# A four-layer graph network on one core: batches between layers 0 and 1, segment maxima inside layer 3's first pass, reciprocals inside its second, and one column for ScalarE

## The chip, the cores and the metric

One NeuronCore of one Trainium2 chip. TensorE (PE in the profile), VectorE (DVE), ScalarE (ACT), GpSimd (POOL) and the queues of SyncE (SP) run side by side and wait for each other by semaphores. A name with a q behind it in the profile (DVEq) is that engine's sequencer: the small steps with which it works out an address in a loop or the value of a wait. The metric is the device time of one execution in microseconds (us).

## The reference: what is computed

```python
h = relu(layernorm(x)); x = x + L0(h)     # weighted sums over neighbours, weights from cosines
h = relu(layernorm(x)); x = x + L1(h)     # 8 relations, softmax over each node's edges per relation
h = relu(layernorm(x)); x = x + L2(h)     # gated messages, their sum and maximum, an MLP
h = relu(layernorm(x)); x = x + L3(h)     # 4 heads:

e = leaky_relu(xl[src] + xr[dst], 0.2)                    # xl, xr: (nodes, 4, 64)
score = einsum('ehc,hc->eh', e, att)                      # (100000 edges, 4)
m = segment_max(score, dst)
ex = exp(score - m[dst])
denom = segment_sum(ex, dst)
alpha = ex / maximum(denom[dst], 1e-16)
out = segment_sum(alpha[:, :, None] * xl[src], dst).mean(axis=1) + bias_gat
# then batch norm, an MLP of 256, batch norm
```

There are 3,125 nodes with 64 values and 100,000 edges sorted by destination. All is float32.

## The kernel before

Node i lies on partition i // 25, so that 25 tiles (NT) hold all nodes; they are worked on in five batches (NBATCH) of five tiles (NB). Edge e lies on partition e // 784 (T = 784 columns), and a loop over edges goes over 98 groups (NG) of 8 columns (K). `quads` unrolls six groups, and then a loop has four groups in its body. Nearly all large tiles are parts of one SBUF tensor, `arena`. `Beats` counts the finished instructions of one kind; its `wait` makes the engine wait for the last of them, its `done` is an instruction and that wait, and `step` is the same with one semaphore for all.

**From layer 0 to layer 1.** VectorE copies the neighbour sums out of PSUM (L1857). TensorE turns them, 25 products for each half of the partitions (L1282), into PSUM banks 0 to 3; VectorE waits for both halves, joins all 25 tiles in two instructions (L1862, L1863), normalises all 25 tiles (`norm_relu`, L1660 to L1668, with a square root on ScalarE, L882), and stages the first batch (L1689). Then for each batch TensorE turns it (L1163), ScalarE lifts it to SBUF (L896), TensorE multiplies it (L1177, five products into bank 5 and then five of 512 columns over banks 0 to 4), and VectorE takes the results (`nodes1`, L1877 to L1882) into one tile, tb1. SyncE writes tb1 to HBM (L587), and `nodes1` of the next batch waits for that.

**Layer 3, first pass.** For each group GpSimd issues eight indirect gathers (L714), and for group g it waits for the `relu3` of group g - 4; SyncE loads another tile (L629), ScalarE writes the gathered rows out again (L1089). In `edges3` VectorE fills eight columns (L1775, an instruction with 260 values a column), and between these, two groups behind, multiplies what TensorE added up (`relu3`, L2251, which waits for TensorE; L1347 and L1348) and reduces it (L2258); three groups behind it writes the scores (`score3`, L2266). A line L110 is the value of a `Beats` wait.

**Between the passes** VectorE works alone. `segment_totals` makes running maxima over the 784 columns of each of four heads (four scans, L1924), carries them over the partitions and back; ScalarE takes the exponentials; `segment_totals` again for the sums. Then the sums f3 (128 x 3136) are bounded below (L2301), inverted (L2302) and multiplied into the scores (L2303).

**Layer 3, second pass.** SyncE loads each group's rows (L655, four buffers). The eight columns of a group are multiplied by their weights (128 x 256 each): five (KD = 5) by VectorE (L2322), three by GpSimd (L826), into y3, which has two buffers. TensorE adds the four heads of the group by four products (L1428, each two records of 512 columns); VectorE, two groups behind, carries a sum in (`sum_in`, L2033) and scans (`sum_up`, L2043). For each pair of groups ScalarE copies marks (L1008), and copies and writes out the states (L996, L998). All that write y3 for group g wait until TensorE has finished group g - 2 (`heads3`), and TensorE waits for `made3` (VectorE) and `made3b` (GpSimd).

```python
                for k in range(KD):
                    makes3.add(dve.tensor_tensor(y3[:, s % 2, k, :]..., gc3[:, s, k, 0:HD]..., ..., ALU.mult))
                    if behind and k == 0:
                        sum_in(sums3, run3, sums_of(s), g - 2, (s - 2) % 4)
                    if behind and k == 2:
                        sum_up(1, sums3, run3, reset3, sums_of(s), g - 2, (s - 2) % 4, before_of(g, s, uses, 2))
```

## Time and profile before

| | us |
|---|---|
| median of 3 runs | 7694.43 (7693.56 to 7702.85) |
| the profiled execution | 7678.81 |
| its span (first to last instruction) | 7677.1 |
| busy in the span: TensorE | 2797.3 (36%) |
| VectorE | 3910.7 (51%) |
| ScalarE | 1035.7 (13%) |
| GpSimd | 3543.8 (46%) |
| mean traffic to and from HBM | 135 GB/s |

The shares are means over stages that differ widely, so they are read by stage. Times in the rows are microseconds from the start of the span, and a duration is that of the instruction without the time for which it waited. Where a row joins several instructions (x3), the duration runs from the first's start to the last's end. Matmul ends are modelled, from when TensorE was given them.

### The profile page before, as it was taken

Reading aid. Unit: us, or ns where it says so; the run is one execution under the profiler, and the core shown is the slowest. Engines: PE = TensorE matmul, PEld = TensorE weight load, DVE = VectorE, ACT = ScalarE, POOL = GpSimd, SP = SyncE. Lnnn points to the kernel's source line nnn. Section 1 sums busy time; section 2 is a strip of 40 time slices with the busy share of each in tenths; the row PEclk is TensorE's granted clock in tenths of the full one; section 3 lists DMA queues with packets and bytes.
Section 4 is the critical chain, followed back from the end, with each engine's and each line's share of the span. In section 5 each row is a group of like instructions: output and inputs, shape, how many; then the busy total and the mean of one; then the engine's idle time right before and its main releaser. Section 6 shows DMA issues by size and latency. Waiting matters only on the chain. (4 is left out here: it accounts for less than half of the span.)

```text
span 7677.1 us, 62689 instructions
## 1 busy us (share of the span) xinstructions
PE 2797.3 (36%) x10695; PEld 1388.6 (18%) x10695; DVE 3910.7 (51%) x10477; ACT 1035.7 (13%) x2409; POOL 3543.8 (46%) x3645
## 2 busy tenths in 40 slices
PE   2116200156600000290003333333345566555695
PEld 1114100012200000280001111111122222222232
DVE  4127200499700000299865455555545666666995
ACT  0000000012100000281352111111110000000232
POOL 5650577300177777400002655555536566654453
PEclk9999999987755555595556666666677877877897
DMA  8100000046321111100242656565637777776593
GB/s 310 44 22 13 10 1 0 0 180 231 115 85 47 47 47 47 26 0 0 101 148 71 227 198 202 196 206 193 203 110 241 243 246 244 248 245 208 208 332 117
DMA packets 458298, 1038.78 MB, mean 135 GB/s; under 512 B 129581, under 2 KB 247829, under 8 KB 428140
## 3 DMA queue, kind: packets, MB, share of 16 engines
q1 hardware_dynamic: 167594, 579.38, 21.3%
q0 software_dynamic: 131968, 217.09, 10.3%
q10 hardware_dynamic: 158658, 241.42, 8.9%
q8 instruction: 31, 0.51, 0.0%
q14 instruction: 47, 0.39, 0.0%
HBM read 559.03 MB, written 476.15 MB: 135 GB/s over the span
## 5 line engine op out<-in xcount | busy, mean ns | idle before, releaser
L714 POOL DMA_INDIRECT arena<-tab,ring x2352 | 2345.6, 997 | 1385.1 <-issue 1132.3
L1347 PE MATMUL psum<-arena,ident 128*128 128x512 f32 x1176 | 759.7, 733 | 1437.0 <-DVE arena L1775 1270.8
L1775 DVE SCALAR_TENSOR_TENSOR arena<-arena,ns 128x64 f32<-128x64 f32 (+2 forms) x2351 | 874.4, 372 | 488.2 <-issue 316.0
L756 POOL DMA_INDIRECT weights<-arena x784 | 772.6, 985 | 386.5 <-issue 332.9
L1907 DVE SCALAR_TENSOR_TENSOR arena<-iota_row,base,psum 128x200 f32<-128x200 f32 x784 | 278.3, 420 | 1083.5 <-remote 1022.5
L1348 PE MATMUL psum<-arena,ident 128*128 128x512 f32 x1176 | 696.2, 677 | 0.0
L1311 PE MATMUL psum<-agg,arena 128*128 128x200 bf16 x2352 | 262.4, 267 | 1049.5 <-issue 554.3
L1347 PEld LDWEIGHTS psum<-arena,ident 128*128 128x128 f32 x1176 | 255.5, 232 | 1832.0 <-issue 1325.6
L703 POOL DMA_INDIRECT put<-arena,zidx x75 | 73.6, 982 | 755.1 <-DVE arena L1882 646.5
L1311 PEld LDWEIGHTS psum<-agg,arena 128*128 128x128 bf16 x2352 | 210.8, 104 | 1087.3 <-issue 599.8
L2251 DVE SCALAR_TENSOR_TENSOR arena<-psum,rowb 128x1024 f32<-128x1024 f32 x196 | 239.0, 1219 | 306.7 <-remote 290.3
L1428 PE MATMUL psum<-arena,ident 128*128 128x512 f32 x784 | 361.7, 607 | 64.1 <-DVE arena L2322 63.7
L826 POOL TENSOR_TENSOR arena<-arena,score 128x256 f32<-128x256 f32 x294 | 232.5, 816 | 272.0 <-issue 121.9
L1565 DVE SCALAR_TENSOR_TENSOR arena<-psum,arena,upper 128x128 bf16<-128x128 f32 x784 | 227.3, 348 | 224.7 <-remote 171.2
L1348 PEld LDWEIGHTS psum<-arena,ident 128*128 128x128 f32 x1176 | 264.8, 225 | 365.5 <-issue 365.5
L2149 DVE SCALAR_TENSOR_TENSOR arena<-arena,ns 128x64 f32<-128x64 f32 x783 | 220.6, 282 | 193.0 <-issue 179.3
L1727 DVE TENSOR_TENSOR nodev<-psum,nodev 128x25 f32<-128x25 f32 x98 | 17.4, 178 | 549.3 <-remote 548.3
L1229 PE MATMUL psum<-arena 128*128 128x25 bf16 x784 | 38.3, 185 | 686.6 <-DVE arena L1737 565.4
L2153 DVE SCALAR_TENSOR_TENSOR arena<-arena,neg 128x64 f32<-128x64 f32 x783 | 218.3, 279 | 136.3 <-issue 126.4
L731 POOL DMA_INDIRECT arena<-betas,eidx x25 | 24.9, 995 | 569.6 <-DVE score L2025 559.2
L932 ACT ACTIVATE psum<-psum,own_row 128x512 f32<-128x512 f32 x196 | 129.8, 662 | 1119.3 <-remote 1068.3
L2258 DVE TENSOR_REDUCE arena<-arena 128x8 f32<-128x512 f32 x392 | 265.3, 678 | 0.1
(422 smaller groups left out, 4669.6 us busy)
## 6 DMA issues: line engine op xcount, KB each, us to landing
put<-zero SPq DMA_DIRECT2D x98, 1040.0 KB
arena<-put SPq DMA_DIRECT2D x98, 1040.0 KB
spill<-arena ACTq DMA_DIRECT2D x98, 1024.0 KB
arena<-spill SPq DMA_DIRECT2D x98, 1024.0 KB
state<-arena ACTq DMA_DIRECT2D x147, 512.0 KB
weights<-zero SPq DMA_DIRECT2D x32, 1600.0 KB
arena<-weights SPq DMA_DIRECT2D x32, 1600.0 KB, 7.5
put<-zero SPq DMA_DIRECT2D x14, 3584.0 KB
```

The source lines that it names most:

```text
L714: pool.indirect_dma_start(out=rows[:, h, k, :], out_offset=None, in_=table[:, :], in_offset=bass.IndirectOffsetOnAxis(ap=ring[:, h, word + ...
L756: pool.indirect_dma_start(out=weights0[:, :], out_offset=bass.IndirectOffsetOnAxis(ap=words0[:, g, k:k + 1], axis=0), in_=words0f[:, g, K ...
L826: message = pool.tensor_tensor(y3[:, s % 2, k, :].rearrange("p (h c) -> p h c", c=D), gc3[:, s, k, 0:HD].rearrange("p (h c) -> p h c", c=D ...
L1311: mm = pe.matmul(bank(2 + 2 * h + k // 2)[:, k % 2 * NT * R:(k % 2 + 1) * NT * R], lhsT=picks[:, h, k, :], rhs=s_parts[:, a, :], start=(a ...
L1347: pe.matmul(place, lhsT=ident[:, :], rhs=rows_of[0][:, s, columns, 0:width], start=True, stop=False)
L1348: mm = pe.matmul(place, lhsT=ident[:, :], rhs=rows_of[1][:, s, columns, 0:width], start=False, stop=True)
L1428: mm = pe.matmul(bank(h).rearrange("p (c k) -> p k c", k=K), lhsT=ident[:, :], rhs=y3[:, h, :, head * D:(head + 1) * D], start=(head == 0) ...
L1565: marked = dve.scalar_tensor_tensor(out=alike[:, h * 4 + k, :], in0=bank(h)[:, k * P:(k + 1) * P], scalar=key[:, column], in1=upper[:, :], ...
L1775: beats.add(dve.scalar_tensor_tensor(out=rows[:, s, k, :], in0=before, scalar=mark(ns, g, k), in1=rows[:, s, k, :], op0=ALU.mult, op1=ALU. ...
L1907: pick = dve.scalar_tensor_tensor(out=sifted[:, h * 4 + k, :], in0=iota_row[:, :], scalar=src_column[:, column], in1=bank(2 + 2 * h + k // ...
L2251: beats3.add(dve.scalar_tensor_tensor(out=pr3[:, columns, :], in0=bank(4 * h + 2 * part, 2).rearrange("p (k c) -> p k c", c=HD), scalar=0. ...
L2258: beats3.add(dve.tensor_reduce(rs3[:, columns, :], pr3[:, columns, :].rearrange("p k (h c) -> p k h c", c=D), AX.X, ALU.add))
```

## The change

In the passage TensorE signals after each five tiles of the second half, so that `join0(b)` and `norm_batch` of one batch can follow; VectorE joins and prepares batch 0, joins the other four, and prepares batch b + 1 ahead of `nodes1(b)`. The first product of layer 1 waits for all five joins, since they read the banks it writes.

In layer 3's first pass the running maxima are made inside `edges3`, three groups behind, by four scans of eight columns, at column 6 of the group; `segment_totals` skips its first four scans.

Behind it only the first ten groups (80 of 784 columns of each head) are bounded, inverted and multiplied; the others follow in the second pass's loop, two groups at a time, four groups ahead, in three instructions of 64 values (`normalise3`), 44 times. VectorE makes four columns of a group, not five; GpSimd still three (4 to 6), and ScalarE the last, in four instructions of 64 values. TensorE and the loads wait for `made3c` too, and GpSimd and ScalarE for `normed3`.

The diff, without the renumbering of the waits for square roots (2 + b becomes 6 + b, and so on) and the declarations of tiles and semaphores:

```diff
@@ -71,8 +71,9 @@
 STEPS3 = 7
+AHEAD3 = 4
 READS3 = 3
-KD = 5
+KD, KP = 4, 7
 AREA = 27780
@@ -652,6 +655,7 @@
                     sp.wait_ge(made3b, g - 3)
+                    sp.wait_ge(made3c, g - 3)
                 sp.dma_start(gc3[:, s, :, :], group_rows(spill3, g)).then_inc(loaded[s], 16)
@@ -822,7 +826,8 @@
                 ready((loaded[s], uses[0] * 16 + 16 * (1 + after(3, s))), *(((heads3, g - 1),) if late(g, 2) else ()))
-                for k in range(KD, K):
+                pool.wait_ge(normed3, max(uses[1], 1) if isinstance(g, int) else uses[1])
+                for k in range(KD, KP):
                     message = pool.tensor_tensor(y3[:, s % 2, k, :].rearrange("p (h c) -> p h c", c=D),
@@ -923,8 +928,9 @@
-            deviation(1)
-            lift_only(1)
+            for b in range(NBATCH):
+                deviation_of(1 + b, b)
+                lift(1, b)
@@ -997,15 +1003,29 @@
-            def pass_sums(use, work, run, reset, table, rows):
+            def messages3(g, s, uses):
+
+                act.wait_ge(loaded[s], uses[0] * 16 + 16 * (1 + after(3, s)))
+                act.wait_ge(normed3, max(uses[1], 1) if isinstance(g, int) else uses[1])
+                if late(g, 2):
+                    act.wait_ge(heads3, g - 1)
+                for k in range(KP, K):
+                    for head in range(H):
+                        message = act.activation(y3[:, s % 2, k, head * D:(head + 1) * D], gc3[:, s, k, head * D:(head + 1) * D],
+                                                 ACT.Copy, scale=score[:, head, bass.ds(g * K, K)][:, k:k + 1])
+                message.then_inc(made3c, 1)
+
+            def pass_sums(use, work, run, reset, table, rows, messages):
...
                         return
+                    messages(g, s, uses)
                     if late(g, 4):
...
                     act.activation(reset[:, s:s + 2, :, 1:K], over(marks.unsqueeze(2), P, 2, D, K - 1), ACT.Copy).then_inc(resets, 1)
+                    messages(g + 1, s + 1, uses)
                     if late(g, 2):
@@ -1279,16 +1299,24 @@
                 for i in range(NT):
-                    mm = pe.matmul(bank(0, 4)[side, i * D:(i + 1) * D], lhsT=by_place[:, i, :], rhs=ident[side, side], start=True, stop=True)
-                mm.then_inc(turned0, 1)
-                pe.wait_ge(turned0, half + 4)
+                    mm = pe.matmul(bank(i // NB)[side, i % NB * D:(i % NB + 1) * D], lhsT=by_place[:, i, :], rhs=ident[side, side], start=True, stop=True)
+                    if half and i % NB == NB - 1:
+                        mm.then_inc(turned0, 1)
+                if half == 0:
+                    mm.then_inc(turned0, 1)
+                    pe.wait_ge(turned0, 4)
...
             pe.wait_ge(consts, 20)
-            products(1, lambda b: mix(1, b, wrel_all, wa_full[:, :, :].rearrange("d a r -> d (a r)")))
+
+            def mix1(b):
+                if isinstance(b, int) and b == 0:
+                    pe.wait_ge(weighted, TILES * 4 + NBATCH)
+                mix(1, b, wrel_all, wa_full[:, :, :].rearrange("d a r -> d (a r)"))
+            products(1, mix1)
             pe.wait_ge(taken, 2 * NBATCH)
@@ -1422,6 +1450,7 @@
                 pe.wait_ge(made3b, g + 1)
+                pe.wait_ge(made3c, g + 1)
                 if not isinstance(g, int) or g >= 2:
@@ -1668,15 +1697,16 @@
-            def norm_batch(use, b):
+            def norm_batch(use, b, squares_of=None):
                 at = bass.ds(b * NB, NB)
+                squared_rows = agg if squares_of is None else squares_of
                 col = [lnv[:, k, at] for k in range(4)]
...
                                               op0=ALU.mult, op1=ALU.add))
-                step(dve.tensor_tensor(agg[:, at, :], hn[:, at, :], hn[:, at, :], ALU.mult))
-                step(dve.tensor_reduce(col[1], agg[:, at, :], AX.X, ALU.add))
+                step(dve.tensor_tensor(squared_rows[:, at, :], hn[:, at, :], hn[:, at, :], ALU.mult))
+                step(dve.tensor_reduce(col[1], squared_rows[:, at, :], AX.X, ALU.add))
                 dve.sem_inc(root_in, 1)
@@ -1857,13 +1887,19 @@
-            dve.wait_ge(turned0, 5)
-            sums = bank(0, 4)[:, 0:NT * D].rearrange("p (i c) -> p i c", c=D)
-            step(dve.scalar_tensor_tensor(out=agg[:, :, :], in0=wh, scalar=sc[:, 6:7], in1=sums, op0=ALU.mult, op1=ALU.add))
-            step(dve.scalar_tensor_tensor(out=xn[:, :, :], in0=agg[:, :, :], scalar=sc[:, 2:3], in1=xn[:, :, :], op0=ALU.mult, op1=ALU.add))
-
-
-            norm_relu(1)
+            def join0(b):
+
+                dve.wait_ge(turned0, 5 + b)
+                at = slice(b * NB, b * NB + NB)
+                sums = bank(b)[:, 0:NB * D].rearrange("p (i c) -> p i c", c=D)
+                dve.scalar_tensor_tensor(out=mixed0[:, at, :], in0=wh[:, at, :], scalar=sc[:, 6:7], in1=sums, op0=ALU.mult, op1=ALU.add).then_inc(weighted, 1)
+                dve.wait_ge(weighted, TILES * 4 + b + 1)
+                step(dve.scalar_tensor_tensor(out=xn[:, at, :], in0=mixed0[:, at, :], scalar=sc[:, 2:3], in1=xn[:, at, :], op0=ALU.mult, op1=ALU.add))
+
+            def prepare1(b):
+
+                norm_batch(1 + b, b, mixed0)
+                stage(1, b, hn)
             beats1 = Beats(dve, node_vec[1], 4)
@@ -1880,7 +1916,14 @@
                     dve.tensor_copy(tb1[:, lo:hi, :, :].rearrange("p j r c -> p (j r) c"), product(lo * R * D, (hi - lo) * R * D, D)).then_inc(used, 1)
-            node_phase(1, hn, nodes1)
+            join0(0)
+            prepare1(0)
+            for b in range(1, NBATCH):
+                join0(b)
+            for b in range(NBATCH):
+                if b < NBATCH - 1:
+                    prepare1(b + 1)
+                nodes1(b)
             dve.wait_ge(taken, 2 * NBATCH)
@@ -1961,11 +2004,11 @@
-            def segment_totals(use, values, totals, n, op, marks, last_marks, spare, at_end, ends=lambda: first_last[:, :], ready=None):
+            def segment_totals(use, values, totals, n, op, marks, last_marks, spare, at_end, ends=lambda: first_last[:, :], ready=None, scanned=False):
...
                 ops = (ALU.add, ALU.max) if op == "max" else (ALU.mult, ALU.add)
-                for r in range(n):
+                for r in range(0 if scanned else n):
                     if ready:
@@ -2264,6 +2307,18 @@
                 dve.tensor_tensor(score[:, :, bass.ds(g * K, K)].rearrange("p h k -> p k h"), rs3, zl3, ALU.add).then_inc(scored, 1)
+
+            maxes3 = Beats(dve, maxed3, H)
+
+            def maximum3(g):
+
+                dve.wait_ge(scored, g + 1)
+                maxes3.group(g)
+                maxes3.wait()
+                at = bass.ds(g * K, K)
+                for h in range(H):
+                    before = -BIG if isinstance(g, int) and g == 0 else f3[:, h, bass.ds(g * K - 1, 1)]
+                    maxes3.add(dve.tensor_tensor_scan(f3[:, h, at], neg[:, at], score[:, h, at], before, ALU.add, ALU.max))
@@ -2279,6 +2334,8 @@
                             reduce3(k - 4)
+                    if late(g, 3) and k == 6:
+                        maximum3(g - 3)
             quads(dve, edges3)
@@ -2288,19 +2345,36 @@
                 score3(g)
-            dve.wait_ge(scored, NG)
+            for g in range(NG - 3, NG):
+                maximum3(g)
+            dve.wait_ge(maxed3, NG * H)
             for s in range(4):
...
-            segment_totals(6, score, f3, H, "max", neg[:, :], lambda: neg_last[:, :], spare3, lambda: penalty(late3))
+            segment_totals(6, score, f3, H, "max", neg[:, :], lambda: neg_last[:, :], spare3, lambda: penalty(late3), scanned=True)
             for r in range(H):
...
             segment_totals(8, score, f3, H, "sum", ns[:, :], lambda: nl[:, :], spare3, lambda: first_last[:, :], ready=lambda r: dve.wait_ge(soft_exp, 3 + r + 1))
-            step(dve.tensor_scalar(f3, f3, 1e-16, None, ALU.max))
-            step(dve.reciprocal(f3, f3))
-            step(dve.tensor_tensor(score, score, f3, ALU.mult))
+            eases3 = Beats(dve, eased3, 4)
+            shares3 = cin[:, 0:H * 2 * K].rearrange("p (h k) -> p h k", h=H)
+
+            def normalise3(use, first):
+
+                at = bass.ds(first * K, 2 * K)
+                eases3.group(use)
+                eases3.done(dve.tensor_scalar(shares3, f3[:, :, at], 1e-16, None, ALU.max))
+                dve.sem_inc(eased3, 1)
+                eases3.k += 1
+                eases3.add(dve.reciprocal(shares3, shares3))
+                eases3.wait()
+                eases3.done(dve.tensor_tensor(score[:, :, at], score[:, :, at], shares3, ALU.mult))
+            lead = slice(0, (6 + AHEAD3) * K)
+            step(dve.tensor_scalar(f3[:, :, lead], f3[:, :, lead], 1e-16, None, ALU.max))
+            step(dve.reciprocal(f3[:, :, lead], f3[:, :, lead]))
+            step(dve.tensor_tensor(score[:, :, lead], score[:, :, lead], f3[:, :, lead], ALU.mult))
+            dve.sem_inc(normed3, (6 + AHEAD3) // 2 - 1)
             dve.sem_inc(ended, 1)
@@ -2326,7 +2400,10 @@
                         sum_up(1, sums3, run3, reset3, sums_of(s), g - 2, (s - 2) % 4, before_of(g, s, uses, 2))
-            quads(dve, edges3c)
+                if not isinstance(g, int) and s % 2 == 0:
+                    normalise3(uses[1] - 3, g + AHEAD3)
+                    dve.sem_inc(normed3, 1)
+            quads(dve, edges3c, apart=AHEAD3)
             for g in (NG - 2, NG - 1):
```

`quads(dve, edges3c, apart=4)` goes over the same 98 groups, with the last four written out behind the loop; `isinstance(g, int)` is true where a group is written out, so `normalise3` is in the loop's body only.

## Rows read from the trace of the kernel before

**Rows 1.** The stages by windows: engines busy (instructions), granted clock, DMA share.

```profile
6000.00:6300.00 300.00, 185.59 (x379) 78.01 (x380) 200.65 (x384) 0.00 (x0) 181.21 (x186) 0.79 0.75 248
...
7163.00:7555.00 392.00, 361.51 (x784) 141.74 (x784) 362.80 (x685) 145.82 (x97) 232.50 (x294) 0.99 0.90 316
```

**Rows 2.** Timeline of the passage: start, duration, instruction, idle time before it.

```profile
2029.06 12.59 PE L1282 MATMUL psum<-ident,agg 64*64 64x64 f32 x100 [1.93 <-DVE agg L1857]
...
2041.76 1.88 DVE L1862 SCALAR_TENSOR_TENSOR agg<-arena,sc,psum 128x1600 f32<-128x1600 f32 x1 [12.76 <-PE psum L1282]
...
2053.43 0.31 DVE L1667 RECIPROCAL lnv<-lnv 128x25 f32<-128x25 f32 x1 [0.44 <-ACT lnv L882]
...
2055.64 0.33 DVE L1689 TENSOR_SCALAR hst<-hn 128x320 f32<-128x320 f32 x1
...
2058.40 2.31 PE L1177 MATMUL psum<-wa,hT 128*128 128x16 f32 x10 [0.79 <-ACT hT L896]
...
2065.36 0.20 DVE L1877 COPY agg<-psum 128x40 f32<-128x40 f32 x1 [7.38 <-PE psum L1177]
...
2073.90 0.20 DVE L1877 COPY agg<-psum 128x40 f32 x1 [4.61 <-DMA tab<-arena]
```

**Rows 3.** Groups of instructions: a step over five tiles, and ScalarE on 64 columns.

```profile
L967 ACT ACTIVATE arena<-arena,score 128x64 f32<-128x64 f32 x784 | 197.6, 334 | 174.6 <-DVE arena L1775 141.4 <-DMA arena<-spill 28.7 <-issue 4.5
...
L1676 DVE SCALAR_TENSOR_TENSOR hn<-lnv,xn 128x320 f32<-128x320 f32 x10 | 4.9, 492 | 0.3
```

**Rows 4.** Chain of waits in layer 3's first pass: start, duration, piece.

```profile
6409.02 0.04 DVEq L110
...
6413.81 0.70 DVEq L1775
...
6415.21 0.69 DVEq L2265
...
6421.52 5.72 another core or an unknown queue
```

**Rows 5.** GpSimd timeline in the same pass, gathers around one stall and the next.

```profile
6422.74 0.95 POOL L714 DMA_INDIRECT arena<-tab,ring  x1 [0.30 <-issue]
6431.51 0.94 POOL L714 DMA_INDIRECT arena<-tab,ring  x1 [7.82 <-DVE arena L2251]
...
6462.31 0.95 POOL L714 DMA_INDIRECT arena<-tab,ring  x1 [0.30 <-issue]
```

**Rows 6.** Lines with their first and last start: layer 3's first pass.

```profile
L2258 DVE TENSOR_REDUCE arena<-arena x392: 670/679/687, 5819.0 to 7077.1; 128x8 f32<-128x512 f32 x196
```

**Rows 7.** The same for layer 2's pass.

```profile
L2153 DVE SCALAR_TENSOR_TENSOR arena<-arena,neg x783: 270/279/355, 4267.8 to 5662.0; 128x64 f32<-128x64 f32 x196
```

**Rows 8.** VectorE timeline between the passes.

```profile
7078.06 7.27 DVE L1924 TENSOR_TENSOR_SCAN arena<-neg,score 128x784 f32<-128x784 f32 x4
...
7137.31 1.79 DVE L2301 TENSOR_SCALAR arena<-arena 128x3136 f32<-128x3136 f32 x1
7139.13 19.75 DVE L2302 RECIPROCAL arena<-arena 128x3136 f32<-128x3136 f32 x1
7158.92 3.43 DVE L2303 TENSOR_TENSOR score<-score,arena 128x3136 f32<-128x3136 f32 x1
```

**Rows 9.** VectorE timeline in layer 3's second pass.

```profile
7302.89 0.42 DVE L2322 TENSOR_TENSOR arena<-arena,score 128x256 f32<-128x256 f32 x1 [0.52 <-PE psum L1428]
...
7305.89 1.10 DVE L2322 TENSOR_TENSOR arena<-arena,score 128x256 f32<-128x256 f32 x3
...
7307.15 1.36 DVE L2322 TENSOR_TENSOR arena<-arena,score 128x256 f32<-128x256 f32 x2
```

**Rows 10.** ScalarE and GpSimd in the same microseconds.

```profile
7306.08 2.07 ACT L996 ACTIVATE arena<-arena 128x1024 f32<-128x1024 f32 x1 [3.90 <-DVE arena L2043]
7306.60 2.38 POOL L826 TENSOR_TENSOR arena<-arena,score 128x256 f32<-128x256 f32 x3 [1.29 <-issue]
```

**Rows 11.** TensorE timeline in the same pass, a pair of groups a row.

```profile
7306.85 7.38 PE L1428 MATMUL psum<-arena,ident 128*128 128x512 f32 x16 [0.51 <-DVE arena L2322]
```

20 lines of the change are left out of this document (11 added, 9 removed).

## The prediction

> **What bounds the kernel now.** I read the stages by windows first. No engine is the bound over the whole span; each stage has its own, so each part of the change is costed at its own place. In layer 3's second pass TensorE is busy for 361.51 us of 392 and VectorE for 362.80, so the two hand work to each other with little to spare [rows 1]. In the first pass no engine is near full: TensorE 185.59 us of 300, VectorE 200.65, GpSimd 181.21, DMA 0.75 [rows 1]. Its limit has to be looked for in the chain of waits and on GpSimd's timeline. The passage and the stretch between the passes are chains of single instructions, read from timelines.
>
> The profiled execution took 7678.81 us, 15.6 less than the median of the three runs, 7694.43. I make the sum against the profiled one and take its difference off the median. A change of 0.2% (15.4 us) is about what a measurement of this kernel can tell from none.
>
> **The passage: -13.** Now VectorE joins at 2041.76, after all 25 turns of the second half, and stages its first batch at 2055.64; TensorE's first product starts at 2058.40, 2.43 after the stage ended [rows 2]. The two halves' turns start at 2029.06 and take 12.59 us, so the first five turns of the second half end at about 2029.06 + 6.30 + 1.26 = 2036.6. Batch 0 then needs two joins and five steps of normalisation over five tiles, seven at 0.49 [rows 3], a trip to ScalarE (0.44), a reciprocal of five columns (under 0.31) and the stage (0.33) [rows 2]: 4.6 us, staged at 2041.3. TensorE must wait for the other four joins, eight instructions at 0.49: 3.9 us, to 2045.2; with 0.4 us for the semaphores the first product starts at 2045.6, 12.8 before now. Batch 0's results, now taken at 2065.36, come as much earlier [rows 2]. The batches behind it are paced by the write of tb1: at 2073.90 VectorE had waited 4.61 for the transfer [rows 2], and the next batch's preparation (5 x 0.49 and the small steps, 3.5 us) lies in that wait. Were it not hidden there, 1 us a batch would go back: -9. If the joins' hops cost nothing, -15.
>
> **The running maxima in the first pass: +28.** The scans taken out behind the pass save 7.27 us [rows 8]. Three groups' scans must follow the loop, some 2 us: tail **-5**. What 98 groups pay for it is the open term. The four scans of eight columns are short: a scan of 784 columns takes 7.27 / 4 = 1.82 [rows 8], so eight columns are 0.02 and a fixed part; a reciprocal of 128 x 25 takes 0.31 [rows 2] where 3136 columns take 19.75 [rows 8], 6.3 ns a column, which leaves 0.15 fixed. So 0.7 us a group, and VectorE has 100 us in 300 idle [rows 1]. If that were all it would be hidden.
>
> The cycle has a place where it is not. The pass takes 7077.1 - 5819.0 = 1258 us for 98 groups, 12.84 each [rows 6], and GpSimd repeats after 6462.31 - 6422.74 = 39.6 us, that is three groups: 24 gathers of 1.3 us and a stall of 7.82 for the multiplication of `relu3` [rows 5]. The chain of waits goes through VectorE's sequencer there: a step of it is 0.04 at 6409.02, but 0.70 at 6413.81 and 6415.21, and the two pieces lie 1.4 us apart [rows 4]. From about 6410 on the steps are slow, through the third group of the cycle, and then comes a piece of 5.72 us with no owner shown, up to 6427.24 [rows 4]. I read it as VectorE waiting for TensorE, which waits for the last gathered rows: GpSimd's last gather before its stall ended at 6422.74 + 0.95 = 6423.69 and the multiplication for which it stalls lets it go on at 6431.51 [rows 5]. So slow steps before that piece are hidden up to 5.72 us and those beyond it lengthen the cycle. `maximum3` adds two waits whose values have to be computed, and at least four places (mark, score, result, the column before) in the sequencer: 6 to 12 steps, I take 8. It stands at column 6, behind which the third group's slow steps begin. 8 x 1.4 = 11.2 us would overrun 5.72 by 5.5, but behind the piece the chain shows no slow steps until the next third group, so what is left of `maximum3` then should run at 0.04 a step. The time lost to a cycle lies between nothing (all steps of it fast or covered) and 4.4 us (two thirds of the overrun and the scans); I take 0.9, the 0.7 us of scans and a few steps: 0.9 x 98 / 3 = +28. Bounds 0 and +145.
>
> By the Trainium skill, "VectorE: DVE Perf Modes", section "The TRN2 errata", an operation out of SBUF carries a fixed extra cost whatever its size, 58 cycles or more (an estimate: 0.06 us each, 24 us of VectorE's time for the 392 small scans where four long ones do). That speaks against cutting the scans up; the rows agree (0.15 fixed), and it costs time only where VectorE is what is waited for.
>
> **The first ten groups' normalisation: -22.** 1.79 + 19.75 + 3.43 = 24.97 us now [rows 8]. 80 of 784 columns of each head are 2.5, with the fixed parts 2.7.
>
> **The second pass: 0, and -4 at its ends.** TensorE does a pair of groups in 7.38 us and waits 0.51 for VectorE's column: 7.89 a pair [rows 11], 8.0 by the window (392 / 49). VectorE waits 0.52 a pair for TensorE [rows 9]. A column alone is 1.10 / 3 = 0.37, beside GpSimd's multiplications 1.36 / 2 = 0.68 [rows 9]. The fifth column of a group comes after the scan, when GpSimd has ended (it multiplies from 7306.60 for 2.38 [rows 10]), so the pair saves 2 x 0.37 = 0.73. `normalise3` costs 0.20 (as the copy of 128 x 40 [rows 2]) + 0.15 + 64 x 0.0063 = 0.55 for the reciprocal + 0.20 + 0.25 for the waits: 1.2. Net +0.47 a pair, into a wait of 0.52: VectorE becomes full and the pair stays at 7.89. ScalarE is busy 145.82 / 49 = 2.98 a pair [rows 1] and gets 8 x 0.334 = 2.67 [rows 3], so 5.7 of 7.89. It starts on the even group's column only when it has copied the states, at 7306.08 + 2.07 = 7308.15 [rows 10]; with the issue of the write it ends at some 7309.8, and TensorE needs it at 7306.85 + 3.69 = 7310.54 [rows 11]: covered by 0.7. The loads' wait for ScalarE ends no later than that for VectorE, GpSimd's share is unchanged, and DMA is busy 0.90 [rows 1]. Five pairs have no `normalise3` and gain up to 0.73 each: -4. Lower bound: TensorE never waits, 44 x 0.51 = -22, and -30 if all its idle time in the window goes [rows 1]. Upper: steps and multiplication delayed by GpSimd make `normalise3` 2.0, +0.8 a pair: +35.
>
> By the Trainium skill, "SBUF — State Buffer", section "Who interferes with whom", a VectorE instruction with two inputs in SBUF contends with GpSimd's reads, and PE and ACT wait for nobody. The rows agree (0.68 beside GpSimd, 0.37 alone). By it ScalarE's column is free, but `normalise3`'s multiplication may be slowed.
>
> **The sum.** -13 + 28 - 5 - 22 + 0 - 4 = **-16**, so 7694.4 - 16 = **7678**.
>
> **The rivals.** (A) The first pass hides the maxima: the slow steps lie elsewhere, or fit into 5.72 us. Everything else stays: -44, 7650. For it speaks VectorE's idle third [rows 1], against it that the chain runs through VectorE's own sequencer [rows 4]. (B) The first pass gets much longer, the case on the other side. From about 2 us beyond the cover, GpSimd's stall comes not once in three groups but oftener, and the pass takes the form that layer 2's has: 5662.0 - 4267.8 = 1394 us, 14.2 a group [rows 7] against 12.84 [rows 6]. Fully that is +137, 7694 - 44 + 137 = 7787; at +2.5 us a cycle, +82, 7732. (C) VectorE is more than full in the second pass: +35 on the forecast, 7713; for it that only 0.05 us a pair is left, against it that the waits in `normalise3` are few. (D) `normalise3` is cheaper, TensorE becomes the bound there: -30, 7648.
>
> **How the numbers follow.** Forecast 0.38, A 0.30, B 0.15, C 0.12, D 0.05. The forecast lies at the edge of what can be told from no change, so its chance is shared: 0.16 faster, 0.20 same, 0.02 slower. A and D are faster, with 0.01 of A for a tie. B is slower, C slower but for 0.02. Faster 0.50, same 0.23, slower 0.27. The range goes from below A (7640) to between B's two forms (7765), and leaves out B's full form and the far ends of A and D. If the likeliest case holds, 7662 to 7692.
>
> **What the next profile would show.** The first row of L1877's successor 13 us earlier. The first pass 1286 us long, not 1258, with slow sequencer steps on the line of the new scan in the chain, 5.72's successor near nothing and GpSimd's stall near 8.7 instead of 7.82; if it is still 1258, A. The stretch between the passes 27 us shorter. The second pass's window 388, with no wait left on VectorE, and ScalarE busy some 130 us more. The forecast is wrong if the sequencer's slow steps are fewer than I count, if the passage's gain is lost to the transfer of tb1 that follows, or if the steps of `normalise3` are as slow as those of the first pass.

## The result, and the profile after

Over 17 executions each, the changed kernel takes a median of 7727.70 us and the kernel before 7702.85 us; the ratio of the two, in which one slow execution of the changed kernel (12131 us) is left out, is 1.0033, with a 95% interval of 1.0020 to 1.0046. So the change makes the kernel slower by about a third of a percent (25 us), where 16 us less were forecast. The profiled execution of after is the one of 7727.70 us, with a span of 7726.0. That of before, at 7678.81, lies 24 under its median, so the two traces differ by 49 us, twice what the medians do. Traces say well in which stage time went, and medians how much in all.

The same four stretches in both traces. The passage is counted from TensorE's first turn to VectorE's first instruction over layer 1's edges; the first pass from the first to the last reduction of `relu3`; the second pass from VectorE's first instruction in it to the addition of the sums behind it:

| stretch | before | after | forecast of the difference |
|---|---|---|---|
| passage, up to the start of layer 1's pass | 87.9 | 72.3 | -13 |
| layer 3's first pass | 1258.8 | 1338.0 | +28 |
| between the passes | 85.0 | 57.8 | -27 |
| layer 3's second pass | 402.5 | 419.1 | -4 |

The first: -15.6; the second: +79.2; the third: -27.2; the fourth: +16.6. What lies between shifts by some microseconds either way in any two executions (layer 2's pass was 1396 and 1387 long). The passage's ends are the first starts of these lines, of before and of after.

```profile
L1907 DVE SCALAR_TENSOR_TENSOR arena<-iota_row,base,psum x784: 416/419/424, 2116.9 to 3474.8; 128x200 f32<-128x200 f32 x196
...
L1950 DVE SCALAR_TENSOR_TENSOR arena<-iota_row,base,psum x784: 414/418/424, 2099.5 to 3458.8; 128x200 f32<-128x200 f32 x196
```

The windows of after: the same stretch of the first pass as in [rows 1], and the second pass.

```profile
6000.00:6300.00 300.00, 171.74 (x360) 71.75 (x359) 201.44 (x444) 0.00 (x0) 171.14 (x177) 0.81 0.70 230
7194.71:7613.80 419.09, 364.45 (x786) 142.25 (x786) 374.19 (x726) 242.69 (x491) 216.35 (x295) 0.98 0.85 297
```

In the 300 us of the first pass VectorE has 444 instructions now and is no busier than before (201.44 against 200.65 [rows 1]), while TensorE and GpSimd have done less (171.74 and 171.14 us against 185.59 and 181.21 [rows 1]): the whole cycle has slowed. In the second pass ScalarE is busy for 242.69 us, and VectorE's 374.19 leave 45 of 419 idle: it is not the full engine that I had expected.

The passage in after's timeline.

```profile
2027.20 12.60 PE L1302 MATMUL psum<-ident,agg 64*64 64x64 f32 x100 [1.93 <-DVE agg L1887]
...
2035.10 0.55 DVE L1895 SCALAR_TENSOR_TENSOR arena<-arena,sc,psum 128x320 f32<-128x320 f32 x1 [7.95 <-PE psum L1302]
...
2039.50 0.33 DVE L1719 TENSOR_SCALAR hst<-hn 128x320 f32<-128x320 f32 x1
...
2043.25 0.55 DVE L1895 SCALAR_TENSOR_TENSOR arena<-arena,sc,psum 128x320 f32<-128x320 f32 x1
...
2043.85 2.32 PE L1197 MATMUL psum<-wa,hT 128*128 128x16 f32 x10 [2.42 <-DVE arena L1895]
...
2050.36 0.20 DVE L1913 COPY agg<-psum 128x40 f32<-128x40 f32 x1 [2.39 <-PE psum L1197]
...
2058.76 0.20 DVE L1913 COPY agg<-psum 128x40 f32<-128x40 f32 x1 [1.24 <-DMA tab<-arena]
```

Batch 0 is joined from 2035.10 on and staged at 2039.50, the last join starts at 2043.25, and TensorE's first product at 2043.85. That is 14.6 ahead of before's [rows 2], but the turns themselves started 1.9 earlier in this trace (2027.20 against 2029.06), so the passage has gained 12.7 up to here, and the forecast was 12.8. The second batch's results are taken at 2058.76 behind a wait of 1.24 for the transfer, where before VectorE waited 4.61 [rows 2]: the preparation does lie in that wait.

The first pass, by the lines of its last reduction and of the new scans (duration min/median/max in ns, first and last start), and GpSimd's timeline.

```profile
L2301 DVE TENSOR_REDUCE arena<-arena x392: 668/679/687, 5798.6 to 7136.0; 128x8 f32<-128x512 f32 x196
...
L2321 DVEq FUSED_REGOPS  x644: 1/93/736, 5870.8 to 7123.1; - x161
L2321 DVE TENSOR_TENSOR_SCAN arena<-neg,arena,score x388: 209/222/235, 5842.0 to 7138.7; - x184, 128x8 f32<-128x8 f32 x10
L2321 DVEq ALU_OP  x92: 6/45/1395, 5871.0 to 7122.3; - x92
```

```profile
6407.91 0.94 POOL L718 DMA_INDIRECT arena<-tab,ring  x1 [10.46 <-DVE arena L2294]
...
6437.30 0.95 POOL L718 DMA_INDIRECT arena<-tab,ring  x1 [0.30 <-issue]
6449.17 0.94 POOL L718 DMA_INDIRECT arena<-tab,ring  x1 [10.92 <-DVE arena L2294]
...
6491.13 0.95 POOL L718 DMA_INDIRECT arena<-tab,ring  x1 [10.13 <-DVE arena L2294]
```

7136.0 - 5798.6 = 1337 us, against 1258 [rows 6]. GpSimd still issues 24 gathers and stalls for `relu3` (L2294 now), but for 10.46, 10.92 and 10.13 us where it was 7.82 [rows 5], so the cycle (from the end of one stall to the end of the next) is 41.3 and 42.0 us and no longer 39.6. The scans themselves are short: 0.22 us, near what was expected. But the address steps of their line, 736 in all (644 and 92) with medians of 0.09 and 0.045 us, reach 0.736 and 1.395.

Between the passes, and the second pass on VectorE and TensorE.

```profile
7136.82 2.14 DVE L2321 TENSOR_TENSOR_SCAN arena<-neg,arena,score 128x8 f32<-128x8 f32 x12
...
7190.89 0.33 DVE L2374 TENSOR_SCALAR arena<-arena 128x320 f32<-128x320 f32 x1
7191.25 2.15 DVE L2375 RECIPROCAL arena<-arena 128x320 f32<-128x320 f32 x1
7193.44 0.49 DVE L2376 TENSOR_TENSOR score<-score,arena 128x320 f32<-128x320 f32 x1
...
7362.74 0.39 DVE L2396 TENSOR_TENSOR arena<-arena,score 128x256 f32<-128x256 f32 x1
7363.05 0.18 DVE L2367 TENSOR_SCALAR cin<-arena 128x64 f32 x1
7363.39 0.55 DVE L2370 RECIPROCAL cin<-cin 128x64 f32<-128x64 f32 x1 [0.15 <-DVEq L2368]
7364.08 0.23 DVE L2372 TENSOR_TENSOR score<-score,cin 128x64 f32 x1
7364.66 0.42 DVE L2396 TENSOR_TENSOR arena<-arena,score 128x256 f32<-128x256 f32 x1 [0.36 <-DVE score L2372]
...
7351.74 3.70 PE L1457 MATMUL psum<-arena,ident 128*128 128x512 f32 x8 [0.88 <-DVE arena L2396]
7355.71 3.69 PE L1457 MATMUL psum<-arena,ident 128*128 128x512 f32 x8 [0.27 <-ACT arena L1014]
7360.16 7.41 PE L1457 MATMUL psum<-arena,ident 128*128 128x512 f32 x16 [0.75 <-DVE arena L2396]
7368.39 3.69 PE L1457 MATMUL psum<-arena,ident 128*128 128x512 f32 x8 [0.83 <-DVE arena L2396]
```

The lead's three instructions end at 7193.93, 3.0 us for what took 24.97 [rows 8]. From the bound at 7363.05 to the next column at 7364.66 are 1.61 us, and 1.80 in the block before it, of which the instructions fill 0.18 + 0.55 + 0.23; the rest are waits of VectorE for its own results. TensorE now waits 0.88, 0.75 and 0.83 for VectorE at every pair of groups, and 0.27 for ScalarE's column between: a pair takes (7368.39 - 7351.74) / 2 = 8.33 us, against 7.89 [rows 11].

### The profile page after: what moved, and what is told of

Same layout as the page of the kernel before. It is cut to its first block and busy times, and to the rows that moved or that the text cites. A ratio compares the mean times of both kernels' runs of the same rounds, so it can differ in the third digit from the quotient of the medians.

```text
span 7726.0 us, 65174 instructions
## 1 busy us (share of the span) xinstructions
PE 2784.8 (36%) x10695; PEld 1382.3 (18%) x10695; DVE 3964.2 (51%) x10931; ACT 1130.5 (15%) x2805; POOL 3517.9 (46%) x3645
## 5 line engine op out<-in xcount | busy, mean ns | idle before, releaser
L1375 PE MATMUL psum<-arena,ident 128*128 128x512 f32 x1176 | 749.0, 724 | 1520.7 <-DVE arena L1805 1406.4
L1376 PE MATMUL psum<-arena,ident 128*128 128x512 f32 x1176 | 686.6, 669 | 0.0
L1457 PE MATMUL psum<-arena,ident 128*128 128x512 f32 x784 | 363.8, 608 | 56.6 <-DVE arena L2396 49.8
L831 POOL TENSOR_TENSOR arena<-arena,score 128x256 f32<-128x256 f32 x294 | 215.4, 759 | 281.0 <-issue 150.7
L2294 DVE SCALAR_TENSOR_TENSOR arena<-psum,rowb 128x1024 f32<-128x1024 f32 x196 | 238.6, 1218 | 48.6 <-remote 33.5
```

The lines of the kernel that those rows point to most:

```text
L1375: pe.matmul(place, lhsT=ident[:, :], rhs=rows_of[0][:, s, columns, 0:width], start=True, stop=False)
L1376: mm = pe.matmul(place, lhsT=ident[:, :], rhs=rows_of[1][:, s, columns, 0:width], start=False, stop=True)
L1457: mm = pe.matmul(bank(h).rearrange("p (c k) -> p k c", k=K), lhsT=ident[:, :], rhs=y3[:, h, :, head * D:(head + 1) * D], start=(head == 0) ...
L2294: beats3.add(dve.scalar_tensor_tensor(out=pr3[:, columns, :], in0=bank(4 * h + 2 * part, 2).rearrange("p (k c) -> p k c", c=HD), scalar=0. ...
```

## The experiments

They ran in five groups, each on one chip beside the kernel before, and the chips are of two kinds. The table counts the steps of VectorE's sequencer (its waits left out) that take over 0.4 us in each trace, and those of them inside the first pass; the last three columns are the stretches of the trace in us. "Before, same chip" is the median of the kernel before in that group.

| | before, same chip | ratio, 95% interval | steps over 0.4 us, all | steps over 0.4 us, in the first pass | first pass | between | second pass |
|---|---|---|---|---|---|---|---|
| before, first trace | 7702.85 | | 736 | 224 | 1258.8 | 85.0 | 402.5 |
| after, first trace | 7702.85 | 1.0033 (1.0020 to 1.0046) | 846 | 437 | 1338.0 | 57.8 | 419.1 |
| e1 no maxima | 5023.15 | 0.9953 (0.9941 to 0.9965) | 0 | 0 | 991.0 | 63.0 | 419.0 |
| e2 maxima alone | 5023.15 | 0.9981 (0.9970 to 0.9991) | 0 | 0 | 990.6 | 79.7 | 403.4 |
| e3 passage alone | 5023.15 | 0.9970 (0.9961 to 0.9980) | 0 | 0 | 994.2 | 85.0 | 402.5 |
| e4 fixed places | 5023.15 | 0.9945 (0.9930 to 0.9960) | 0 | 0 | 992.8 | 57.0 | 417.4 |
| e5 maxima in pairs | 5027.15 | 0.9959 (0.9944 to 0.9974) | 0 | 0 | 990.6 | 57.1 | 418.7 |
| e6 maxima early | 5027.15 | 0.9964 (0.9950 to 0.9977) | 0 | 0 | 1001.0 | 57.8 | 418.3 |
| e7 normalisation spread | 5027.15 | 0.9954 (0.9941 to 0.9967) | 0 | 0 | 1001.4 | 63.1 | 411.1 |
| e8 column alone | 5027.15 | 0.9957 (0.9945 to 0.9968) | 0 | 0 | 1001.3 | 85.1 | 389.0 |
| e9 changed again | 7631.24 | 1.0046 (1.0029 to 1.0064) | 836 | 422 | 1297.1 | 57.8 | 418.8 |
| e10 before again | 7631.24 | | 597 | 115 | 1242.7 | 85.0 | 402.7 |
| e11 blocks alone | 7631.24 | 1.0013 (1.0001 to 1.0024) | 536 | 116 | 1230.0 | 63.1 | 457.1 |
| e12 column and maxima | 7631.24 | 1.0046 (1.0028 to 1.0064) | 842 | 442 | 1319.6 | 79.8 | 389.5 |
| e13 changed, third | 7682.34 | 1.0017 (1.0001 to 1.0033) | 813 | 417 | 1314.9 | 57.8 | 418.6 |
| e14 column again | 7682.34 | 0.9943 (0.9923 to 0.9964) | 608 | 219 | 1256.8 | 85.1 | 389.3 |
| e15 fixed again | 7682.34 | 0.9945 (0.9927 to 0.9963) | 732 | 297 | 1241.6 | 57.1 | 418.9 |
| e16 pairs again | 7682.34 | 0.9946 (0.9928 to 0.9965) | 765 | 375 | 1261.2 | 57.1 | 418.4 |
| e17 pairs and column | 7688.64 | 0.9937 (0.9916 to 0.9959) | 801 | 360 | 1266.9 | 79.1 | 389.1 |
| e18 early again | 7688.64 | 0.9963 (0.9950 to 0.9976) | 888 | 426 | 1287.0 | 57.8 | 418.6 |

The times of e1 to e8 are compared with each other only and with the 5023 or 5027 us of the kernel before on their chips.

A stretch of a single trace is no exact measure. Layer 2's pass, which no run changes, is between 1359 and 1400 us long in the four traces e13 to e16 of one chip, and the first pass, which is the same code in e9 and e12, is 1297.1 and 1319.6. Differences of some 20 us between two traces say nothing by themselves, so the medians are asked beside them.

**e1, no maxima in the first pass.** The scans of 784 columns are back behind the pass.

```diff
-                    if late(g, 3) and k == 6:
-                        maximum3(g - 3)
...
-            for g in range(NG - 3, NG):
-                maximum3(g)
-            dve.wait_ge(maxed3, NG * H)
+            dve.wait_ge(scored, NG)
...
-            segment_totals(6, score, ..., scanned=True)
+            segment_totals(6, score, ...)
```

> The changed kernel, but with the running maxima made behind the first pass again by four scans of 784 columns; all else of the change stays. Theory (the small scans' sequencer steps lengthen each cycle of three groups by some 2.5 us): the first pass goes from 1337 us between its first and last reduction back to 1258, the stretch behind it is 5 us longer, and the whole is some 74 us shorter than the changed kernel, 50 below the kernel before (ratio 0.994). Rival (the first pass got longer for another reason, such as the passage's new batches or the order of transfers): the first pass stays above 1300 and the time stays at that of the changed kernel.

**e2, the maxima alone,** put into the kernel before (`maximum3`, its call at column 6, `scanned=True`).

> The kernel before with the maxima inside the first pass and nothing else of the change. Theory: first pass 1258 to 1337, the scans behind it 5 us less, so 74 us slower than before (ratio 1.0096). Rival (the loss needs the other parts too): under 40 us.

**e3, the passage alone,** the kernel before with `join0`, `prepare1` and what belongs to them.

> The kernel before with the passage from layer 0 to layer 1 in batches and nothing else of the change. Theory: layer 1's first product 14.5 us earlier, and still 13 to 17 us earlier where layer 3 starts: ratio 0.998. Rival (given back to the writes and waits of the later stages): earlier by under 5 us from layer 2 on, ratio 1.000.

**e4, fixed places.**

```diff
-                at = bass.ds(g * K, K)
                 for h in range(H):
-                    before = -BIG if isinstance(g, int) and g == 0 else f3[:, h, bass.ds(g * K - 1, 1)]
-                    maxes3.add(dve.tensor_tensor_scan(f3[:, h, at], neg[:, at], score[:, h, at], before, ALU.add, ALU.max))
+                    maxes3.add(dve.tensor_tensor_scan(f3[:, h, 0:K], neg[:, 0:K], score[:, h, 0:K], -BIG, ALU.add, ALU.max))
```

> The changed kernel, but the four small scans of a group always work on the first eight columns of each head and start from a constant, so that their addresses need no steps in the sequencer; waits, number of scans and columns stay (the maxima, and with them the weights, are those of wrong columns). Theory (address steps at 0.7 us each in the slow stretch are the price): the first pass falls from 1337 to some 1275 us. Rival A (VectorE's time for the scans, or the wait for the score ahead of them): it stays above 1320. Rival B (the two waits with computed values are most of it): 1300 to 1320.

The chip was another than that of the first traces: the kernel before took 5023 us there. e1 and e2 missed their numbers (990.6 us for the first pass with the maxima, 991.0 without, and no loss of 74 us): on this kind of chip the maxima cost nothing that shows, and e2 is even 0.19% faster, of which the 5.3 us less behind the pass are 0.11%. The line of the scans in e2 shows what differs.

```profile
L2279 DVEq FUSED_REGOPS  x644: 65/93/124, 3457.8 to 4390.8; - x161
L2279 DVE TENSOR_TENSOR_SCAN arena<-neg,arena,score x388: 209/218/294, 3438.9 to 4408.6; - x184, 128x8 f32<-128x8 f32 x10
L2279 DVEq ALU_OP  x92: 45/45/45, 3458.0 to 4390.1; - x92
```

As many steps, 644 and 92, but none above 0.124 us, where after's reached 0.736 and 1.395; the scans take the same 0.22 us. The chain of waits of e2's first pass goes through GpSimd's gathers one behind the other and not through VectorE's sequencer.

```profile
3807.33 0.94 POOL arena L715
3808.27 0.30 issue
3808.58 0.95 POOL arena L715
3809.53 0.30 issue
...
3827.59 6.78 DMA arena<-tab,ring
```

A gather and its issue are 1.25 us, and 784 of them 980 of the 991 us: the pass is paced by GpSimd's gathers (the DMA engines are busy for 0.91 of it, against 0.69 in after's), and some 1.6 us more on VectorE a group (an estimate: four scans of 0.22 and 8.4 steps of 0.09) lie beside it. So e4 could tell nothing apart on this chip (992.8). e3's ratio of 0.9970, 15 us of 5023 (10 to 20 by its interval), agrees with the theory that the passage's gain stays, though layer 3 starts only 7 us earlier in its trace than in e2's (3409.2 against 3416.0).

**e5, the maxima of two groups at a time,** every second group, in four scans of 16 columns: half as many steps, waits and scans.

```diff
...
-                at = bass.ds(g * K, K)
+                at = bass.ds(g * K, 2 * K)
...
-                    if late(g, 3) and k == 6:
-                        maximum3(g - 3)
+                    if late(g, 4) and s % 2 == 0 and k == 6:
+                        maximum3(g - 4, uses[1] - 2)
...
```

> The changed kernel, but the maxima of two groups are made at once, every second group, in four scans of 16 columns: as many columns, half as many steps, waits and scans. Theory (the sequencer's steps are the price, per instruction): the first pass takes half of the 79 us it lost, about 1297 us. Rival (once the cycle is longer at all it keeps its longer form, or a block of steps in one group costs as much as one in each): 1325 or more.

**e6, the maxima early:** `k == 2` in place of `k == 6`.

> The changed kernel with the small scans behind column 2 instead of column 6 of a group. Theory (the whole third group of a cycle runs with slow steps, so the column doesn't matter): first pass 1337 as at column 6, within 15 us. Rival (column 6 is the unlucky place, as the prediction argued): it falls to 1258 to 1290.

**e7, the normalisation spread** over the columns of the even group, on e1.

```diff
...
-                if not isinstance(g, int) and s % 2 == 0:
-                    normalise3(uses[1] - 3, g + AHEAD3)
-                    dve.sem_inc(normed3, 1)
+                    if not isinstance(g, int):
+                        if s % 2 == 0 and k >= 1:
+                            normalise3(uses[1] - 3, g + AHEAD3, k - 1)
+                        if s % 2 and k == 0:
+                            eases3.wait()
+                            dve.sem_inc(normed3, 1)
```

> e1 (no maxima in the first pass), and the three instructions of the normalisation in the second pass stand behind columns 1, 2 and 3 of the even group instead of one behind the other at its end, with their waits covered by the columns between. Theory (the block costs 1.8 us of which 0.8 are waits for its own results; VectorE is the limit): the period of a pair falls from 8.3 us to about 7.6 to 7.8, the second pass by some 25 us against e1. Rival (GpSimd's multiplications are slowed or delayed by more work of VectorE beside them, or ScalarE's column, for which TensorE waits 0.27, is the limit): under 8 us.

**e8, the column alone,** on e1.

```diff
-            lead = slice(0, (6 + AHEAD3) * K)
-            step(dve.tensor_scalar(f3[:, :, lead], f3[:, :, lead], 1e-16, None, ALU.max))
...
+            step(dve.tensor_scalar(f3, f3, 1e-16, None, ALU.max))
...
-                if not isinstance(g, int) and s % 2 == 0:
-                    normalise3(uses[1] - 3, g + AHEAD3)
-                    dve.sem_inc(normed3, 1)
```

and so on for the other two instructions; `normed3` is raised to 49 at once.

> e1 without the blocks: all 3136 weights are normalised ahead of the second pass as in the kernel before, VectorE makes four columns and ScalarE one. Theory: VectorE has 0.73 us less a pair and TensorE becomes the limit, at 7.38 to 7.6 us a pair: the second pass about 365 to 375 us instead of 392 before and 408 after; 22 us come back ahead of it. Rival (ScalarE's column is late behind the copy of the states, 7.9 or more a pair): no gain against the 392 of the kernel before.

Again a chip without long steps, so e5 and e6 told nothing of the maxima's price. e7 is a half miss: the second pass is 411.1 us, 8 less than e1's, not 25. Its VectorE waits for TensorE again, 0.78 us, 0.32 and 0.78 in three pairs; the waits for its own results are gone, but TensorE still waits 0.98 us for a column of the even group, in which all of the block's work stands. The block's multiplication took 0.63 us where GpSimd multiplied beside it (at 4787.76) and 0.20 where it did not (at 4795.86). By the Trainium skill, "SBUF — State Buffer", section "Who interferes with whom", VectorE's second input out of SBUF contends with GpSimd's reads, and the trace agrees. e8 gave 389.0, 13 less than before; its TensorE is the limit.

```profile
4755.58 7.39 PE L1457 MATMUL psum<-arena,ident 128*128 128x512 f32 x16 [0.27 <-DVE arena L2391]
4763.25 7.37 PE L1457 MATMUL psum<-arena,ident 128*128 128x512 f32 x16 [0.28 <-ACT arena L1014]
...
4755.54 0.43 DVE L2391 TENSOR_TENSOR arena<-arena,score 128x256 f32<-128x256 f32 x1 [0.30 <-PE psum L1457]
...
4759.44 0.42 DVE L2391 TENSOR_TENSOR arena<-arena,score 128x256 f32<-128x256 f32 x1 [0.51 <-PE psum L1457]
```

A pair of groups takes 7.67 us: 7.39 of products and 0.27 of waiting, once for VectorE and once for ScalarE. The 365 to 375 that I expected of e8 was too low, as it left out that wait (0.28 x 49 = 14) and the ends.

**e9 and e10, both kernels again.**

> The changed kernel itself, on a chip of the experiments. In the parts run so far no step of a sequencer took over 0.4 us, where in the two traces first taken 736 (before) and 846 (after) of VectorE's did. Theory (the maxima cost time only where the steps are slow): first pass 990 to 1002 us as without them, the gap behind it 57, the second pass 418; with the passage's 12 that is 5.3 + 22 + 12 - 16 = 23 to 27 us less than the kernel before, ratio 0.995. Rival (the maxima cost time on any chip): ratio 1.000 or above.

> The kernel before itself, for its trace on such a chip: no step of a sequencer over 0.4 us; first pass 990 to 1002 us, second pass 402 with a pair of groups at 7.9 us; if the steps are slow here again (as in the first trace), first pass 1258.

**e11, the blocks alone:** e1 with `KD, KP = 5, 8` and nothing by ScalarE.

> e1 (passage in batches, no maxima in the first pass) with five columns by VectorE again and none by ScalarE; the normalisation in blocks stays. Theory (a block takes 1.8 us of VectorE, which is full): a pair 7.4 + 1.8 = 9.2 us less what VectorE waited, 9.0 to 9.2: the second pass 402 + 44 x 1.2 = 455 us, that is 36 more than with ScalarE's column, against the 22 saved ahead of it. Rival (the blocks hide in VectorE's waits): 402 to 420.

**e12, the column and the maxima:** the changed kernel with e8's edit.

> The changed kernel without the blocks: passage in batches, maxima in the first pass, ScalarE's column, and one normalisation of all weights ahead of the second pass. Theory: gap 85 - 6 = 79 us, second pass 389 as in e8, first pass as in e9; where the steps are fast, 474 - 6 = 468 us behind the first pass against 475 for the changed kernel, so 5 to 8 us faster than e9. Rival (equal, since the blocks pay for themselves): within 2 us.

This chip has long steps, and the result of the first traces came again: 1.0046. The numbers of e9 and e10 for a chip without them did not come (e10's first pass, 1242.7 us, lies near its other case, 1258); e9's theory (the maxima cost time only where the steps are long) is borne out by the first passes. Between its four kernels the parts separate. The first pass is 1230.0 and 1242.7 us without maxima, with 116 and 115 long steps; 1297.1 and 1319.6 with them, with 422 and 442. The blocks cost what was worked out: the second pass of e11 is 457.1 (expected 455).

```profile
7304.99 7.34 PE L1453 MATMUL psum<-arena,ident 128*128 128x512 f32 x16 [1.73 <-DVE arena L2388]
7313.99 7.33 PE L1453 MATMUL psum<-arena,ident 128*128 128x512 f32 x16 [1.66 <-DVE arena L2388]
```

9.0 us a pair, of which TensorE waits 1.7 for VectorE. 457.1 - 402.5 = 54.6 us for 44 blocks are 1.24 each beyond the 0.5 that was idle, against the 22 saved ahead of the pass. e12 gave those 22 back and gained the 29 of the second pass, yet its median is no better than e9's. In its trace the first pass is 22 us longer than in e9's, though the code of that pass is the same, so the 5 to 8 us by which e12 was to be faster are lost in scatter and were not seen.

**e13 to e16, on a fourth chip.**

> The changed kernel itself once more, beside the next three on one chip. If this chip's sequencers have slow steps (over 0.4 us), as in the first traces and in e9: first pass 1295 to 1340 us with over 400 of them, ratio 1.003 to 1.005. If they have none, as in e1 to e8: first pass 985 to 1002, ratio 0.995. Rival (the slow steps have nothing to do with it): a ratio that does not go with their number.

> e8 once more: passage in batches, scans behind the first pass, all weights normalised at once, ScalarE's column. Theory: it has none of the two parts that cost, so it is faster than before on any chip: 12 us by the passage and 13 by the second pass, 25 in all: ratio 0.9967 where the kernel takes 7630 us, and 0.995 where it takes 5020. Rival (where steps are slow the later stages shift by as much as is gained): ratio above 0.999.

> e4 once more: the changed kernel with the small scans at fixed addresses. Where steps are slow: theory (the address steps, some 6 of a group's 8 or 9, are the price): first pass within 20 us of that without maxima (1230 to 1260), slow steps 120 to 200 in it; rival A (the scans themselves and the wait for the score): as the changed kernel, 1297 to 1338; rival B (the waits' values alone): about 1280. Where steps are fast: 990 to 1002 as in e4, nothing told apart.

> e5 once more: maxima of two groups at a time, half the steps. Where steps are slow: theory first pass midway, 1265 to 1295, some 270 slow steps in it; rival (a cycle of three groups now meets a double block of steps every second time, and loses as much): as the changed kernel. Where steps are fast: 985 to 1002 as in e5.

Long steps again, and this is the group that decides. e15 does what the changed kernel does but for the address steps of the scans (its scans read the wrong columns, so its result is not the layer's), and is 0.55% faster than before, where the changed kernel is 0.17% slower. The lines of its last reduction and its scans, then those of e16:

```profile
L2301 DVE TENSOR_REDUCE arena<-arena x392: 671/681/692, 5779.1 to 7020.0; 128x8 f32<-128x512 f32 x196
...
L2319 DVE TENSOR_TENSOR_SCAN arena<-neg,score x392: 154/165/214, 5812.5 to 7022.1; 128x8 f32<-128x8 f32 x196
```

```profile
L2301 DVE TENSOR_REDUCE arena<-arena x392: 672/681/687, 5821.0 to 7081.5; 128x8 f32<-128x512 f32 x196
...
L2321 DVEq FUSED_REGOPS  x345: 2/93/1396, 5889.9 to 7059.0; - x173
L2321 DVE TENSOR_TENSOR_SCAN arena<-neg,arena,score x192: 223/236/303, 5891.0 to 7083.5; - x184, 128x16 f32<-128x16 f32 x8
```

e15 has no step on the scans' line and 392 scans as before; its first pass takes 1242 us, 15 less than e14's 1256.8 without any maxima. With 297 long steps against 219 it loses nothing. e16 has half of the scans' steps (345 and 23 of 736), 375 long ones, and 4 us more than e14. The changed kernel has 417 and 58 us more. The medians say the same: with the differences of the other two stretches taken off, e13's first pass costs 57 us more than e14's and e16's 5, and e15's costs 3 less (the intervals are some 15 us either way). So the waits and the scans of e15 cost nothing that shows. Its scans are shorter than the changed kernel's, 0.165 us against 0.22, as they start from a constant; for 392 scans that is 22 us, which can't make up for 57.

The price is not in proportion to the steps. In the cycles of 24 gathers of e14, e15, e16 and e13 there are 7.0, 10.2, 12.4 and 13.8 long steps, and GpSimd's stall is 7.9, 8.1, 8.4 and 10.2 us. Most of the added steps cost little and the last ones nearly all, as a cover that is used up would have it; where the edge lies these four points can't say. GpSimd's waits for `relu3` in the first pass say the same (us in all, times, longest), first e13, then e15:

```profile
POOL arena L718 <- DVE arena L2294: 293.9, 38, 10.9
...
POOL arena L718 <- DVE arena L2294: 236.9, 38, 8.6
```

**e17, pairs and column,** and **e18, early again.** e17 is e5 with e8's edit: no blocks.

> The parts that gained or cost nothing, together: passage in batches, maxima of two groups at a time in the first pass, ScalarE's column, all weights normalised at once. Theory: 6 us less behind the first pass than e14 (gap 79 instead of 85), second pass 389, first pass as without maxima or up to 15 us longer where steps are slow: ratio 0.993 to 0.997 on either kind of chip. Rival (half the steps still overrun the cover on some chips): first pass 30 us or more above that of the kernel before, ratio 0.999 or above.

> e6 once more: the changed kernel with the small scans behind column 2. Where steps are slow: theory (the whole third group runs with slow steps, the place in it doesn't matter): first pass 1295 to 1340 us and over 400 slow steps. Rival (column 6 is the unlucky place): 1230 to 1270. Where steps are fast: 985 to 1002, nothing told apart.

e17 beats both kernels, 0.63% under the kernel before, and so does e14, 0.57% (and 0.43% on a chip without long steps, as e8). e14's 44 us are more than the 13 of the second pass and the 15 of the passage, and what gave the rest isn't known. e18 came out between the two theories: 426 long steps, as many as at column 6, but a first pass of 1287.0 us, 20 more than e17's on the same chip, where the changed kernel's was 54 more than e16's on the other. e18's ratio, 0.9963, lies below 1, and e18 is the changed kernel in all but the place. So the place seems to matter, and the number of long steps alone doesn't set the loss; but the changed kernel itself did not run on this chip, so this is not shown.

Misses in these two groups: e13's ratio (1.0017, expected 1.003 to 1.005), e14's (0.9943, expected 0.9967), the long steps of e15 (297, expected 120 to 200) and of e16 (375, expected 270), and e16's first pass (1261, expected 1265 to 1295).

## Why the prediction was wrong

**The passage** was right: counted from the start of the turns, the first product came 12.7 us earlier and the first results 13.1, where 12.8 were worked out, and layer 1's pass 15.6, where the forecast kept 13. By e3's ratio the gain stays.

**The scans behind the pass and the lead's normalisation** were right: 85.0 to 57.8 is 27.2 us less, forecast 5 + 22.

**The maxima in the first pass: the step that failed.** The mechanism stands in the prediction (address steps in VectorE's slow stretch overrun the time that it waits for TensorE), and e15 shows that the steps are the price: the same kernel without those of the scans loses none of it. The step that failed is the size of a term, "the time lost to a cycle", taken as 0.9 us. It measured 79.2 / 32.7 = 2.4 in the first pair of traces, (1297.1 - 1242.7) / 32.7 = 1.7 in e9 against e10, and 58 / 32.7 = 1.8 in e13 against e14; by the medians of the first pair it is (25 + 15.6 + 27.2 - 16.6) / 32.7 = 1.6, so 2.4 is partly the chance of those two traces. (0.9 x 98 / 3 is also 29 and not 28, which changes nothing.) The count of steps was right: 2715 - 1887 = 828 more in the pass, 8.4 a group, where I took 8. The assumption under it was not: that only a few of the steps would fall where they count, the rest of `maximum3` running fast behind the 5.72 us of waiting. Each trace has 30 cycles of 24 gathers, and in their mean the long steps now go from 14.0 to 33.6 us after the cycle's first gather, where before it was from 18.2 to 27.6, and there are 14.1 of them a cycle and not 7.2. VectorE begins the third group of a cycle at 35.7 us and no longer at 20.7, so that the slow stretch falls on the second group's steps, and I had counted the third's. The stall of GpSimd is 10.4 us in the mean of these cycles, against 8.0. I had this case as a point of rival B, "+2.5 us a cycle, +82, 7732", and gave B as a whole 0.15. B's full form, stalls oftener than once in three groups, did not come.

**The second pass: the other step that failed.** "Net +0.47 a pair, into a wait of 0.52" is wrong, because `normalise3` costs 1.6 to 1.8 us and not 1.2: I put 0.25 for its waits, and they are 0.15 + 0.14 + 0.36 = 0.65; its multiplication takes 0.23 or, in the block before, 0.42. A pair takes 8.33 us and not 7.89. This lies inside the bounds of the prediction (2.0 and +35); measured are +16.6 with the ends, where -4 were forecast. Nor was ScalarE's column covered by 0.7 us: TensorE waits 0.27 for it in each pair. Its instructions are cheaper than I took them (four in 1.06 us, not 4 x 0.334), so that ScalarE is busy 97 us more and not 130. With e11 (a block beside five columns) and e8 (the column alone) the two parts of the sum are separate: the column takes 13 us off the pass, the block puts 55 on it where VectorE is full, and 30 where ScalarE's column has made room (419.1 against 389.0).

**What I did not see** is that the price of the maxima was found on one kind of chip only. The long steps were in the trace, and I took them for a property of the kernel. Where there are none, all parts of the change together are a gain: e4, e5 and e6, whose steps, waits or place differ from the changed kernel's only where nothing is lost, gave 0.9945, 0.9959 and 0.9964. The changed kernel itself did not run on such a chip, so its ratio there was not measured.

**Not settled:** what makes the sequencer's steps long. They come in VectorE's and SyncE's sequencers (846 and 563 steps over 0.4 us in after's trace) and hardly in the others', and in four of this study's six groups of runs, never in the other two. What owns the wait of 5.72 us that covers them [rows 4] was not found either. Why e18's long steps cost less than those at column 6 wasn't tried further either.

## What to carry to other kernels

In a loop whose addresses are computed, count sequencer steps as work of their own: on the chips with long steps 8.4 of them a group cost 54 to 79 us in single traces and 51 to 57 by the medians, where the same number of scans at fixed addresses cost none, and on the others they cost nothing that shows. Look in the trace for the longest step, not the median, and ask which wait still covers it: half of the steps fitted below that cover here and were nearly free, and the rest made nearly all of the loss. Work of tiny size that is cut out of one long instruction pays its waits for its own results again each time (22 us in one piece, 55 in 44 blocks beside a full VectorE), so give the relief (ScalarE's column) without the blocks, as e14 and e17 do.

## What the runs showed of the hardware

The same kernel took 7631 to 7703 us in four groups of runs and 5023 to 5027 in two, each group on one chip. In the two, no register or address step of VectorE's or SyncE's sequencer took over 0.4 us; in the four, hundreds did, of 0.70 us in the median. Layer 3's first pass without the maxima was 991 to 1001 against 1230 to 1259 us, layer 2's pass 985 to 991 against 1352 to 1400, layer 1's first 293 to 294 against 1356 to 1363, and the second pass of layer 3 the same on both to a microsecond (402.5 and 402.7 on the one, 402.5 on the other). The long steps do not account for all of that difference: in after's trace VectorE also has 122 gaps of over 5 us without any record, 2275 us together, and in e1's 35 with 306.
